# The output stage after attention: reciprocals spread by TensorE, half of its inputs and the gate prepared during attention

## The reference

```python
scores = jnp.where(causal, einsum('bhqd,bhkd->bhqk', Q, K), -inf)
attn = softmax(scores)
s = einsum('bhqk,bkhd->bqhd', attn, V).reshape(B, S, D) @ Wo.T + bo
g = silu(moe(xn))              # silu(F) = F * (1 + tanh(F / 2)) / 2
x = x + s * g
```

## Time and profile before

| what | value |
|---|---|
| time, median of 3 runs (lowest, highest) | 2378.97 us (2376.59, 2379.52) |
| the profiled execution: own time, span | 2376.8 us, 2375.0 us |
| TensorE, VectorE, ScalarE, GpSimd busy, share of the span | 90%, 77%, 51%, 60% |
| 2210 to 2300 us: TensorE, VectorE busy | 83.4, 57.8 of 90 us |
| 2300 to 2345 us: TensorE, VectorE busy | 5.4, 12.9 of 45 us |
| 2345 to 2375 us: TensorE, VectorE busy | 15.9, 24.3 of 30 us |

### The profile page before, as it was taken

One profiled execution on the slowest core, in us unless ns is written; L12 is line 12 of the kernel. 1 busy time (PEld: TensorE's weight loads), 2 busy tenths in 40 slices (PEclk: granted clock), 3 DMA queues, 4 the chain that ended last, 5 costly groups with the idle time before them and its releaser, 6 DMA issues. The chain is left out here.

```text
span 2375.0 us, 40392 instructions
## 1 busy us (share of the span) xinstructions
PE 2145.3 (90%) x13482; PEld 1681.4 (71%) x13482; DVE 1833.0 (77%) x3270; ACT 1206.3 (51%) x2547; POOL 1422.1 (60%) x1467
## 2 busy tenths in 40 slices
PE   4995799999999999999999999978978998999972
PEld 2785688888888888888888888867766775344332
DVE  4885799999999999999999999845753445887745
ACT  1332456665666666666666666534432332566660
POOL 3543478678777877786777777735333333998000
PEclk9997799999999999999999999979988998899996
DMA  2002000000000000000000000044115554333224
GB/s 96 1 14 78 33 3 3 34 3 3 34 3 34 3 3 34 3 3 34 3 12 26 3 3 3 3 148 153 60 60 146 177 178 137 106 118 116 79 63 160
DMA packets 76894, 128.98 MB, mean 54 GB/s; under 512 B 22332, under 2 KB 54684, under 8 KB 74684
## 3 DMA queue, kind: packets, MB, share of 16 engines
q1 hardware_dynamic: 69827, 107.65, 13.4%
q0 software_dynamic: 6864, 18.75, 3.2%
HBM read 91.82 MB, written 46.92 MB: 58 GB/s over the span
## 5 line engine op out<-in xcount | busy, mean ns | idle before, releaser
L976 DVE SCALAR_TENSOR_TENSOR mix_cv<-mix_pp,mix_cw,mix_cv 128x384 f32<-128x384 f32 (+4 forms) x864 | 492.8, 570 | 27.7 <-ACT mix_cv L897 6.2
L821 PEld LDWEIGHTS mix_pyd<-mix_xdt,mix_lm 128*128 128x128 f32 x2048 | 247.4, 192 | 56.7 <-DVE mix_lm L1023 29.0
L78 PE MATMUL mix_pp<-l0in_XH,mix_wx_lo 128*128 128x384 f32 (+2 forms) x576 | 238.0, 413 | 39.1 <-DVE mix_ss L965 25.4
L897 ACT ACTIVATE mix_cv<-mix_pp,mix_cb,mix_cw 128x384 f32<-128x384 f32 (+1 forms) x288 | 182.3, 633 | 175.0 <-PE mix_pp L80 175.0
L821 PE MATMUL mix_pyd<-mix_xdt,mix_lm 128*128 128x64 f32 x2048 | 242.7, 272 | 2.6 <-DVE mix_lm L1023 2.6
L748 POOL TENSOR_TENSOR mix_t<-mix_t,mix_xd 128x512 f32<-128x512 f32 x112 | 144.4, 1289 | 146.7 <-DVE mix_t L1032 146.0
L1935 DVE TENSOR_REDUCE att_tops<-att_psc 128x1 f32<-128x512 f32 (+3 forms) x384 | 189.6, 549 | 47.6 <-PE att_psc L1883 32.2
L1959 ACT ACTIVATE att_pr<-att_pst 128x1024 f32<-128x1024 f32 (+7 forms) x256 | 156.6, 657 | 103.5 <-PE att_pst L1900 73.5
L760 POOL TENSOR_TENSOR mix_xdt<-mix_xtok,l_dt 128x512 f32<-128x512 f32 x128 | 133.9, 1046 | 105.8 <-ACT mix_xtok L926 105.7
L903 ACT ACTIVATE mix_pp<-mix_cv 128x384 f32<-128x384 f32 (+1 forms) x288 | 135.3, 470 | 103.9 <-DVE mix_cv L976 101.3
L80 PE MATMUL mix_pp<-l0in_XH,mix_wx_hi 128*128 128x384 f32 (+2 forms) x576 | 187.7, 326 | 0.0
(11 more groups left out here) (396 smaller groups left out, 6401.7 us busy)
## 6 DMA issues: line engine op xcount, KB each, us to landing
mix_w_raw<-in_w_in SPq DMA_DIRECT2D x8, 1280.0 KB, 5.5
y_d<-exp_ys SPq DMA_DIRECT2D x79, 128.0 KB, 1.8
a_part<-att_sums SPq DMA_DIRECT2D x32, 256.0 KB, 5.3
mix_ll<-cs SPq DMA_DIRECT2D x384, 4.0 KB
q<-q SPq DMA_DIRECT2D x12, 512.0 KB, 4.5
k<-k SPq DMA_DIRECT2D x12, 512.0 KB, 4.6
att_qs<-q SPq DMA_DIRECT2D x32, 192.0 KB
att_ks<-k SPq DMA_DIRECT2D x32, 192.0 KB
```

What stands on the lines that cost most here:

```text
L78: pe.matmul(out, l_lo, r_hi, start=start, stop=False)
L821: last = pe.matmul(pyd[:, h * HP:(h + 1) * HP], lm[p % 2][:, h, :], xdt[p % 2][:, h * HP:(h + 1) * HP], start=True, stop=True)
L897: act.activation(conv_tile(k), pp[k % 2][:, halo:cols], ACT.Identity, bias=cb[:, it // 2, ct:ct + 1], scale=cw[:, it // 2, ct, 3:4]).then_ ...
L976: last = dve.scalar_tensor_tensor(out, of, cw[:, g, ct, 3 - d:4 - d], out, ALU.mult, ALU.add)
```

## The change

- The four tanh move into ScalarE's stream of attention steps 23 to 26, ahead of the step's exponentials (`TANH_AT`). They wait until GpSimd has added all 64 rows.
- After its gather work GpSimd finishes the gate, four tiles of rows at a time: 0.5 * (1 + tanh), times F, then the bias times the gate added to the residual. It then adds the first sequence's partial results.
- SyncE loads the residual, the bias, a selection matrix and the weights in step 6 (`X_AT`), and one of the four parts of the first sequence's results in each of steps 22 to 25 (`FIRST_AT`), each time behind the step's row transfer.
- VectorE splits the weights and takes the first sequence's reciprocals after its last head.
- In the output stage the way of the reciprocals over DRAM is gone. TensorE multiplies them with the 0/1 matrix `sel` (fp32, four matmuls of 128 columns a block) into PSUM banks `pR`, from which VectorE forms the quotient. Only the second sequence's parts are loaded there, four transfers by SyncE and four by ScalarE. Matmuls of a pair of tiles share a bank; VectorE multiplies it with the gate, and GpSimd adds the product to the residual.

```diff
+        bias, gb = s.sb("bias", [P, D]), s.sb("gb", [P, 4, D])
+        x_in, first_in, th_done, opened, gated, biased, summed, tot_v = (
+            s.sem(n) for n in ("x_in", "first_in", "th_done", "opened", "gated", "biased", "summed", "tot_v"))
+        tiles = [slice(b * 4, b * 4 + 4) for b in range(4)]
+        X_AT, FIRST_AT, TANH_AT = 6, 22, 23
+        first = A[:, :, :].rearrange("p k (s f t) -> p k s f t", s=2, f=2)[:, :, 0]
...
+                    if n == X_AT:
+                        sp.dma_start(X[:, :, :], x_d.rearrange("(n p) d -> p n d", p=P)).then_inc(x_in, 16)
+                        sp.dma_start(bias[:, :], bo.partition_broadcast(P)).then_inc(x_in, 16)
+                        sp.dma_start(sel[:, :, :, :], c_sel).then_inc(x_in, 16)
+                        sp.dma_start(w[:, :, :], wo.rearrange("(k p) n -> p k n", p=P)).then_inc(x_in, 16)
+                    if n == FIRST_AT:
+                        for o in range(2):
+                            sp.wait_ge(stored[o], 16 * H1 // 2)
+                    if 0 <= n - FIRST_AT < 4:
+                        j = n - FIRST_AT
+                        sp.dma_start(tot[0:P // 2, j, :], a_part[j, DH, :, 0, :].rearrange("h (b t) -> h b t", b=4)).then_inc(first_in, 16)
+                        for k in range(KD):
+                            to = first[:, k, j] if j < 2 else more[j - 2][:, k, 0]
+                            sp.dma_start(to, a_part[j, k * 8:(k + 1) * 8, :, 0, :].rearrange("c h t -> (c h) t")).then_inc(first_in, 16)
...
+                pool.wait_ge(x_in, 64)
+                for i, r in enumerate(tiles):
+                    pool.wait_ge(th_done, i + 1)
+                    pool.tensor_scalar(th[:, r, :], th[:, r, :], 1.0, 0.5, ALU.add, ALU.mult).then_inc(opened, 1)
+                    pool.wait_ge(opened, i + 1)
+                    pool.tensor_tensor(th[:, r, :], th[:, r, :], F[:, r, :], ALU.mult).then_inc(gated, 1)
+                    pool.wait_ge(gated, i + 1)
+                    wait(pool, summed, i)
+                    pool.tensor_tensor(gb[:, :, :], th[:, r, :], bias[:, :].unsqueeze(1).to_broadcast([P, 4, D]), ALU.mult).then_inc(biased, 1)
+                    pool.wait_ge(biased, i + 1)
+                    pool.tensor_tensor(X[:, r, :], X[:, r, :], gb[:, :, :], ALU.add).then_inc(summed, 1)
+                pool.wait_ge(first_in, 16 * 12)
+                for j in range(2):
+                    pool.tensor_tensor(first[:, :, 1], first[:, :, 1], more[j][:, :, 0], ALU.add).then_inc(joined0, 1)
+                    pool.wait_ge(joined0, j + 1)
...
+                    if n == 0:
+                        dve.memset(rec[P // 2:, :, :], 0.0)
+                dve.wait_ge(x_in, 64)
+                dve.tensor_copy(wh[:, :, :], w[:, :, :]).then_inc(wo_split, 1)
+                dve.wait_ge(wo_split, 1)
+                dve.tensor_tensor(wl[:, :, :], w[:, :, :], wh[:, :, :].bitcast(F32), ALU.subtract).then_inc(wo_split, 1)
+                dve.wait_ge(first_in, 16 * 12)
+                early = slice(0, P // 2)
+                for j in range(2, 4):
+                    dve.tensor_tensor(tot[early, 1, :], tot[early, 1, :], tot[early, j, :], ALU.add).then_inc(tot_v, 1)
+                    dve.wait_ge(tot_v, j - 1)
+                dve.reciprocal(rec[early, :, :], tot[early, 0:2, :]).then_inc(wo_split, 1)
...
+                    if 0 <= n - TANH_AT < len(tiles):
+                        act.wait_ge(joined, NPAIR)
+                        act.activation(th[:, tiles[n - TANH_AT], :], F[:, tiles[n - TANH_AT], :], ACT.Tanh, scale=0.5).then_inc(th_done, 1)
...
+        def part(j, k):
+            return a_part[j, k * 8:(k + 1) * 8, :, 1, :].rearrange("c h t -> (c h) t")
         with nc.Block() as block:
             @block.sync
             def _(sp):
                 for j in range(4):
+                    sp.dma_start(tot[P // 2:, j, :], a_part[j, DH, :, 1, :].rearrange("h (b t) -> h b t", b=4)).then_inc(tot_in, 16)
                 for f in range(2):
+                    for k in range(KD):
+                        sp.dma_start(second[:, k, f], part(f, k)).then_inc(a_in, 16)
+                for b in range(NB):
+                    sp.wait_ge(summed, 2 * (b + 1))
+                    sp.dma_start(out[:, 4 * b:4 * b + 4, :], X[:, 4 * b:4 * b + 4, :]).then_inc(stored, 16)
                 sp.wait_ge(stored, 16 * NB)
             @block.scalar
             def _(act):
+                for j in range(2):
+                    for k in range(KD):
+                        act.dma_start(more[j][:, k, 1], part(2 + j, k)).then_inc(more_in, 16)
                 for b in range(NB):
                     act.wait_ge(quot, b + 1)
                     act.activation(ah[:, :, blocks[b]], A[:, :, blocks[b]], ACT.Copy).then_inc(hi, 1)
+            @block.gpsimd
+            def _(pool):
+                for q in range(PAIRS):
+                    pool.wait_ge(product, q + 1)
+                    pool.tensor_tensor(X[:, 2 * q:2 * q + 2, :], X[:, 2 * q:2 * q + 2, :], S1[q % 2][:, :, :], ALU.add).then_inc(summed, 1)
+            @block.vector
+            def _(dve):
+                def quotient(b):
+                    dve.wait_ge(spread, b + 1)
+                    dve.tensor_tensor(A[:, :, blocks[b]], A[:, :, blocks[b]],
+                                      pR[b % 2][:, :].unsqueeze(1).to_broadcast([P, KD, TB]), ALU.mult).then_inc(quot, 1)
+                def low(b):
+                    dve.wait_ge(hi, b + 1)
+                    dve.tensor_tensor(al[:, :, blocks[b]], A[:, :, blocks[b]], ah[:, :, blocks[b]].bitcast(F32),
+                                      ALU.subtract).then_inc(lo, 1)
+                def gate(q):
+                    dve.wait_ge(mm, q + 1)
+                    if q >= 2:
+                        dve.wait_ge(summed, q - 1)
+                    dve.tensor_tensor(S1[q % 2][:, :, :], py[q % 4][:, :].rearrange("p (t d) -> p t d", t=2),
+                                      th[:, 2 * q:2 * q + 2, :], ALU.mult).then_inc(product, 1)
+                dve.wait_ge(joined0, 2)
+                quotient(0)
+                quotient(1)
+                low(0)
+                low(1)
+                dve.wait_ge(tot_in, 64)
+                late = slice(P // 2, P)
+                for j in range(2, 4):
+                    dve.tensor_tensor(tot[late, 1, :], tot[late, 1, :], tot[late, j, :], ALU.add).then_inc(tot_v, 1)
+                    dve.wait_ge(tot_v, j - 1)
+                dve.reciprocal(rec[late, :, :], tot[late, 0:2, :]).then_inc(inv, 1)
+                gate(0)
+                dve.wait_ge(a_in, 16 * 4)
+                dve.wait_ge(more_in, 16 * 4)
+                for j in range(2):
+                    dve.tensor_tensor(second[:, :, 1], second[:, :, 1], more[j][:, :, 1], ALU.add).then_inc(joined, 1)
+                    dve.wait_ge(joined, j + 1)
+                gate(1)
+                quotient(2)
+                quotient(3)
+                gate(2)
+                low(2)
+                low(3)
+                for q in range(3, PAIRS):
+                    gate(q)
             @block.tensor
             def _(pe):
+                def reciprocals(b):
+                    s_, f = divmod(b, 2)
+                    if s_:
+                        pe.wait_ge(inv, 1)
+                        pe.wait_ge(quot, b - 1)
+                    for c in range(4):
+                        last = pe.matmul(pR[b % 2][:, c * P:(c + 1) * P], sel[:, s_, c, :], rec[:, f, :], start=True, stop=True)
+                    last.then_inc(spread, 1)
+                def products(q):
+                    pe.wait_ge(lo, q // 2 + 1)
+                    if q >= 4:
+                        pe.wait_ge(product, q - 3)
+                    for t in (2 * q, 2 * q + 1):
+                        rows = slice(t * P, (t + 1) * P)
+                        for k in range(KD):
+                            last = matmul3(pe, py[q % 4][:, t % 2 * D:(t % 2 + 1) * D], ah[:, k, rows], al[:, k, rows], wh[:, k, :],
+                                           wl[:, k, :], k == 0, k == KD - 1)
                     last.then_inc(mm, 1)
+                pe.wait_ge(wo_split, 3)
+                reciprocals(0)
+                reciprocals(1)
+                for q in range(4):
+                    products(q)
+                reciprocals(2)
+                reciprocals(3)
+                for q in range(4, PAIRS):
+                    products(q)
...
+    sel = np.zeros((2, H1, 4, 2, 4, 8, H1), np.float32)
+    for h in range(H1):
+        for s_ in range(2):
+            for b in range(4):
+                sel[s_, h, b, s_, b, :, h] = 1
+    sel = sel.reshape(P, 2, 4, P)
```

More of the change, by code:

```diff
@@ L1744, in _, with attention @@
                         dve.tensor_copy(ys[e % NX_RING][:, :], py[e % 2][:, 0:D]).then_inc(y_done, 1)
-def attention(nc, q6, k6, V, a_part, ident, mask_kq, y_d, slot, wts, F, qk_stored):
+def attention(nc, q6, k6, V, a_part, ident, mask_kq, y_d, slot, wts, F, qk_stored,
```

(26 more changed lines are left out.)

83 lines of the change are left out of this document (6 added, 77 removed).

## The result

The changed kernel takes 2361.72 us (median of 4 runs, 2359.91 to 2365.14), the kernel before 2377.78 beside it (4 runs): ratio 0.993, interval 0.9918 to 0.9943. That is 16.1 us less, where 26 were forecast; the predicted 2353 is 8.7 too low. The time lies inside the range of 2344 to 2363, near its upper edge, and outside the forecast's own case of 2348 to 2359. The profiled execution took 2360.87 us, its span 2359.1.

What follows compares the result with a forecast made beforehand. Bound: TensorE with its partners during attention, then transfers and VectorE for 65.5 us. Output stage -32.4 and attention +6.4 give net -26.0: 2376.8 becomes 2350.8, plus 2.2 for the median, 2353 us; range 2344 to 2363.

Steps and rivals of the forecast that it cites:

- the forecast's own case: Whole kernel: the predicted net gain of 26.0 us holds, time 2348 to 2359 us, chance 0.60.
- The bound and the first spread: Output stage start: transfers and VectorE bound it; without DRAM, TensorE's spread of reciprocals comes 1.4 us after the first transfer.
- The stage, -32.4: Output stage, first transfer to end: 65.5 us falls to 33.1, bounds -38 to -27.
- Transfers of step 6, 1.0 (0 to 6): Attention: 2.9 MB issued ahead of head 8's loads make TensorE wait 1.0 us, bounds 0 and 6.
- The far estimate: Step 6 loads: head 8 lands at some 2077, from the residual's 14.4 us until landing in company.
- the near one: Step 6 loads: head 8 lands at 2071, from 7 us for 2.9 MB at 420 GB/s.
- the loads of step 6 come too late: Rival in attention: 6 us of waiting for head 8's loads instead of 1, time 2358; chance 0.05.
- GpSimd's gate, 1.5 (0 to 12): Attention: GpSimd's long operations delay VectorE's small ones, some 1.5 us in step 27 and around the joins, bounds 0 and 12.
- The first rival: Attention: GpSimd's long operations stretch three of the longer steps by 4 to 5 us each, time 2363; chance 0.15.
- Tanh, 3.9: Attention steps 23 to 26: four tanh on ScalarE add 3.9 us, bounds 2.0 and 3.9, without table exchange.
- Slower than before: Rival in attention: all five small operations of a step wait for whole GpSimd operations, four steps giving 2387; chance 0.02.
- all hidden: Rival: attention hides nearly all and the clock stays up, stage -36, attention +2, time 2345; chance 0.15.

Runs made afterwards that it cites:

- the first two experiments: Changed kernel with step 6's loads spread over six steps, 2353.49 us; changed kernel with GpSimd's two first-sequence additions held behind step 28's small operations, 2359.70 us.
- the first experiment: Changed kernel with the residual loaded in four 512 KB pieces in steps 6 to 9, selection matrix, bias and weights in steps 10 and 11: 2353.49 us.
- three edits: Changed kernel with step 6's loads spread, tanh ahead of the last exponential, and GpSimd's two first-sequence additions held behind small operations: 2345.11 us.
- the tanh in a gap: Changed kernel with each tanh ahead of the last exponential of steps 22 to 25 instead of the first of steps 23 to 26: 2357.29 us.
- the gate in the way: Changed kernel with GpSimd's four gate tiles each started later in its step, so they run while VectorE's small operations are due: 2368.81 us.

## Why the prediction was right in direction and too large in size

Of the forecast 26.0 us the two later stretches of the profile show 20.1: attention paid 14.85 instead of 6.4, and the stage gave 34.9 instead of 32.4, so two errors in part cancelled. That the time lies in the range is partly luck: it is 1.3 us inside the edge, and one of the four runs (2365.14) lies beyond it.

- *The bound and the first spread.* Right: first quotient 1.28 us after T (1.4), first product 4.9 (5.1), and the spread without DRAM shortens the stage on its own by 14.2. Both starts went by the high clock. In the profiles of the first two experiments, with the same output stage, TensorE was at 1.2 GHz from T on, the first product came at T + 6.2, and the stage took 31.5. So 0.9 us of the 34.9 is the clock of this execution and not sure to come with the change.
- *The stage, -32.4.* -34.9, inside its bounds; the stage took 30.6 instead of 33.1. Mis-sized: "at the low clock for 5.8 us". TensorE had the high clock when the products began, fell 0.55 us later (2333.95) and rose after 3.2 us; so pairs 0 to 3 took 7.3 instead of 8.3. Pairs 4 to 7 took 7.5, 0.8 less than 8.3. The path in the middle was another than the sum's: the spread of block 2 began at T + 12.2 and was not waited for, since VectorE, held up by the landing at T + 9.9 and by one addition of GpSimd (0.8 us in the joins), was through with gate 1 only at T + 13.8; the sum had TensorE at T + 14.1. The products resumed at T + 17.9, where it had 18.4 without any hold-up and 19 with half of one.
- *Transfers of step 6, 1.0 (0 to 6).* **This is the step that failed**: 7.0, outside its bounds, and undoing it alone gave 7.0 back. The far estimate had the landing of head 8 nearly right: 2077 by the clock of before, 2077.9 measured. That is partly luck: the residual, whose 14.4 us the estimate took, landed after 8.6, and three more loads and an issue 1.3 us later made up the rest. I took 1.0, nearly all from the near one, 7 us at the full rate. And its bound left out that a TensorE that has stood 4.5 us works on at 1.2 GHz: 2.5 us more. The rival "the loads of step 6 come too late" had a chance of 0.05 and should have been the forecast. Without the burst the time falls into the forecast's own range (2353.5, the first experiment).
- *GpSimd's gate, 1.5 (0 to 12).* 4.1, all of it from the joins, where it was expected, at two hits and the low clock after them. That the four tiles would be free was right, with wrong lengths behind it: tensor_scalar took 1.04 instead of 2.9, each multiplication 2.36 instead of 1.89, the four operations of a tile 8.1 instead of 9.1. The 1.89 came from a row of another form: there one factor is repeated over the 256 elements of each row. The first rival is real, as a start 4.6 us later in the step showed.
- *Tanh, 3.9.* 3.76, and no table exchange. The transfers of steps 22 to 25 cost nothing, as forecast.
- *Slower than before; all hidden.* Neither came. With three edits attention hides all but 1.46.
- *The median.* The two later stretches give -20.1, the measured medians -16.1 to -16.6. The difference is the first row of the table: +4.2 ahead of the change's work in attention. Over the profiles of this study the row transfer of step 5 lies between 2052.4 and 2060.4 us, and both ends are variants of the changed kernel with the same code ahead of it, so most of it changes from execution to execution; whether a part belongs to the change was not settled.

The Trainium skill ("SBUF — State Buffer", section "Who interferes with whom") lets the second of two such instructions wait for the whole of the first. The hits agree: 2.19 to 2.28 us where a small operation began just behind a GpSimd operation of 2.35 to 2.39, up to 1.85 where it began later, each to the end of GpSimd's, and none where the operations do not meet.

## What to carry to other kernels

Price a stall of TensorE in the middle of a full pipeline as the wait and the low clock behind it, here 4.5 + 2.5 and 2.6 + 1.4 us. Load bulk data in pieces that fit between two of the pipeline's own transfers, here 512 KB a step, and put GpSimd's long operations just behind VectorE's short ones, with a wait that keeps them there. And run a change's main idea alone: here it gave 14.2 of 20.1 us by the profiles and all that the medians show. What was built around it paid clearly, by 17.9 us more in the medians, only once most of its cost in attention had been removed.

## What the runs showed of the hardware that I had not expected

GpSimd's tensor_scalar with two constants took 1.04 us on 128x1024, against 0.95 for 128x256 with a scalar for each partition. Its multiplications took 2.36, as long as additions. What made 1.89 of it in the earlier trace rows is a factor repeated along the innermost elements; the same holds at 128x512 in the kernel before, 1.05 with such a factor (L760) against 1.29 for two full tensors (L748).

SyncE's issue of the bias, repeated over 128 partitions, took 2.28 us behind the residual's 2 MB, where its neighbours took 0.42 to 0.47. It is not the repetition alone: with the residual loaded in pieces, steps earlier, the same issue took 0.42, and 0.46 in the kernel before.

VectorE's small operations beside GpSimd's long ones are mostly held alternately: one to the end of the GpSimd operation, the next free at 0.17, the one after caught by the following; two in a row were held in two places (after 2254.00 with the tanh in a gap, after 2257.90 with the gate in the way).
